# The split steps of a unit in two groups of four and five instead of three groups: a two-layer interaction network on Trainium2

## The reference

```
x0 = e                                                    # B, 39, 16
z0 = einsum('bid,bjd->bdij', x0, x0)    -> B, 16, 39*39
cur0 = relu(z0 @ W0)                    -> B, 128, 16     # W0: 1521 x 128
next_h, direct0 = split(cur0, 2)        # 64 rows each
z1 = einsum('bid,bjd->bdij', x0, next_h) -> B, 16, 39*64
cur1 = relu(z1 @ W1)                    -> B, 128, 16     # W1: 2496 x 128
z = sum(concat([direct0, cur1]), over the 16)
h = relu([z, dense_ctx] @ W_top1 + b_top1); h = relu(h @ W_top2 + b_top2); y = h @ W_top3
```

## Time and profile before

| | |
|---|---|
| runs | 1511.45, 1515.13, 1517.09 us |
| profiled execution | 1511.94 us; span 1510.1 us |
| busy: TensorE, VectorE, ScalarE, GpSimd | 95%, 92%, 55%, 62% |
| mean granted TensorE clock | 0.979 (below 1 only in the first slices) |
| chain that ended last | TensorE 90%, VectorE 4% |

### The profile page before, as it was taken

One profiled execution on the slowest core, in us unless ns is written; L12 is line 12 of the kernel. 1 busy time (PEld: TensorE's weight loads), 2 busy tenths in 40 slices (PEclk: granted clock), 3 DMA queues, 4 the chain that ended last, 5 costly groups with the idle time before them and its releaser, 6 DMA issues.

```text
span 1510.1 us, 15015 instructions
## 1 busy us (share of the span) xinstructions
PE 1434.6 (95%) x4458; PEld 794.5 (53%) x4458; DVE 1393.3 (92%) x1253; ACT 825.2 (55%) x897; POOL 939.0 (62%) x604
## 2 busy tenths in 40 slices
PE   3179999999999999999999999999999999999999
PEld 2145555555555555555555555555555555555556
DVE  2179999999999999999999999999999999999993
ACT  0155555655655555655655555655655555655555
POOL 7638888868687786868687786868687780000000
PEclk7589999999999999999999999999999999999999
DMA  5069989999989899999989999899998998898510
GB/s 150 6 160 203 227 216 218 206 220 212 221 198 222 206 217 214 208 223 201 220 203 216 214 212 220 208 213 203 212 216 223 212 210 216 204 222 207 170 35 1
DMA packets 137289, 293.08 MB, mean 194 GB/s; under 512 B 37646, under 2 KB 62878, under 8 KB 137080
## 3 DMA queue, kind: packets, MB, share of 16 engines
q1 hardware_dynamic: 102642, 278.48, 77.2%
q0 software_dynamic: 19200, 4.95, 2.9%
q10 hardware_dynamic: 15366, 8.70, 2.1%
HBM read 284.08 MB, written 7.87 MB: 193 GB/s over the span
## 4 chain that ended last, share of the span: by engine, by line
PE 90%; DVE 4%; issue 2%; another core or an unknown queue 2%; ACT 0%; DMA 0%; DVEq 0%; SPq 0%
PE psB L493 42%; PE psA L493 14%; PE psB L511 7%; PE psB L514 6%; PE psB L518 6%; PE psA L501 2%; PE psA L511 2%; PE psA L514 2%; PE psA L518 2%; PE psB L501 2%; DVE z L902 1%; PE psA L485 1%; DVE z_lo L911 1%; DVE z_split L902 1%
## 5 line engine op out<-in xcount | busy, mean ns | idle before, releaser
L472 POOL DMA_INDIRECT emb<-in_tbl,ids_all x600 | 938.8, 1565 | 309.7 <-issue 178.9
L493 PE MATMUL psB<-z,w 128*128 128x512 f32 x1544 | 690.1, 593 | 5.3 <-DVE z L902 5.3
L767 ACT ACTIVATE z_hi<-z_split 128x1024 fp32r<-128x1024 f32 (+1 forms) x286 | 301.4, 1057 | 464.9 <-DVE z_split L902 372.4
L493 PEld LDWEIGHTS psB<-z,w 128*128 128x128 f32 x1544 | 292.4, 190 | 362.7 <-issue 346.0
L902 DVE TENSOR_TENSOR z<-h_quad,x_lay 128x1024 f32<-128x1024 f32 x354 | 420.5, 1218 | 7.4 <-PE psB L493 5.4
L911 DVE TENSOR_TENSOR z_lo<-z_split,z_hi 128x1024 fp32r<-128x1024 f32 (+1 forms) x286 | 349.3, 1221 | 6.3 <-ACT z_hi L767 3.2
L902 DVE TENSOR_TENSOR z_split<-h_quad,x_lay 128x1024 f32<-128x1024 f32 x222 | 268.4, 1221 | 0.0
L720 ACT ACTIVATE h_quad<-psA 32x1024 f32<-32x1024 f32 x248 | 251.7, 1015 | 6.1 <-DVE feat_side L987 2.4
L493 PE MATMUL psA<-z,w 126*128 126x512 f32 x512 | 241.9, 594 | 0.0
L511 PE MATMUL psB<-z_hi,w_hi 128*128 128x512 f32 x444 | 157.7, 436 | 0.0
L493 PEld LDWEIGHTS psA<-z,w 126*128 126x128 f32 x512 | 97.3, 190 | 98.4 <-issue 92.7
(11 more groups left out here) (113 smaller groups left out, 862.5 us busy)
## 6 DMA issues: line engine op xcount, KB each, us to landing
x_lay<-x_rows SPq DMA_DIRECT2D x1152, 128.0 KB
x_more<-x_rows SPq DMA_DIRECT2D x62, 504.0 KB
bases<-x_rows SPq DMA_DIRECT2D x62, 468.0 KB
x_lay<-x_rows SPq DMA_DIRECT2D x64, 256.0 KB
x_ring<-x_rows SPq DMA_DIRECT2D x31, 504.0 KB
emb<-in_tbl,ids_all POOLq DMA_INDIRECT x600
x_last<-x_rows SPq DMA_DIRECT2D x64, 128.0 KB
x_rows<-x_side ACTq DMA_DIRECT2D x58, 120.0 KB
```

The costliest lines, as they stand in the source:

```text
L472: nc.gpsimd.indirect_dma_start(emb[t % 2][:, f * D:(f + 1) * D], None, tables[f], bass.IndirectOffsetOnAxis(ids_all[:, t, f:f + 1], 0)).th ...
L493: mm = nc.tensor.matmul(ps[:, cs], w[0:k, :], z[WHOLE_NO[place] % NZ][0:k, cs], start=first, stop=last)
L767: nc.scalar.activation(z_hi[n % NS][0:k, 0:cols], z_split[n % NS][0:k, 0:cols], ACT.Copy).then_inc(z_hi_made, 1)
```

## The change

Only constants change. The steps that are split, and two places of layer 0:

```diff
-SPLIT0 = (1, 4)
+SPLIT0 = (1, 5)
 HALF1 = 12
-SPLIT1 = (2, 3, 7, 8, 9, 13, 14)
+SPLIT1 = (2, 3, 4, 8, 9, 10, 11)
 WHOLE0 = tuple(s for s in range(STEPS0) if s not in SPLIT0)
-EARLY = (2, 3)
+EARLY = (2, 3, 4)
 WHOLE1 = tuple(s for s in range(STEPS1) if s not in SPLIT1 or s in EARLY)
 ORDER0 = SPLIT0 + WHOLE0
-AFTER = (0, 1, 3, 5, 7, 9, 11)
+AFTER = (0, 1, 4, 5, 7, 9, 11)
 FIRST_AFTER = (1, 3, 4, 5, 7, 9, 11)
```

## The result

The changed kernel takes 1570.51 us in the median of four runs (1568.58 to 1598.4) against 1516.11 us (1511.45 to 1526.23): ratio 1.0345, 95% interval 1.0278 to 1.0412. It is slower by 54 us. The profiled execution took 1572.18 us, 60.2 us above the profiled one of before.

What follows compares the result with a forecast made beforehand. TensorE was taken to bound the kernel, without a gap in its 42.5 us units. Waits of 1.47 and 0.55 us a unit, taken as 1.92, gave 55.7 us over 29 units, 57 in all: 1571 us, range 1548 to 1588.

Steps and rivals of the forecast that it cites:

- first wait: At step 4, TensorE waits for parts delayed by ScalarE's two stores: 1.47 us a unit, 1.36 at the lower end.
- first rival: ScalarE's high part of step 4 is not held by the stores; +12 to +17, 1530 us; chance 0.06.
- group of five: Second group, five split steps: fourth low part costs 0.2 us, fifth 0.36 more; together 0.55 us a unit.
- cut from 2.02 to 1.92 us a unit: Sum of both waits per unit, taken as 1.92 because the 0.1 us extras need not all come.
- open weight load: On TensorE after a real wait: a weight load that nothing hid, costing another 0.1 us.
- boundaries at nothing: Between groups of split and whole steps: changing between fp32 and fp32r costs TensorE 0, so one group fewer saves nothing.
- exit from the half steps: Behind the two half steps, an fp32 step now follows: no change taken, between 0.12 us saved and 0.06 us more.
- second rival: Faster: exit into an fp32 step hides its weight load, 0.12 us in 31 units; lead suffices everywhere; 1511 us; chance 0.03.
- third rival: No change: TensorE has room and makes the waits good, weight loads busy only 53%; 1515 us; chance 0.03.
- fourth rival: Worse: later products hold back loads and VectorE loses lead; 1 us more a unit, 1603 us; chance 0.06.
- Unit 1: Unit after the start, where the lead is short: 0.5 us added to the sum.

Runs made afterwards that it cites:

- e1: Changed kernel with ScalarE's high part of step 4 put ahead of keep_x (copy and two stores): unit 42.84 us, 1485.42 us, ratio 1.0063 to before.
- e6: Changed kernel with only keep_x's two stores moved behind the high part of step 4, the copy staying ahead: unit 42.84 us, ratio 1.0070 to before.
- e7: Changed kernel with one more copy of 120 x 512 into a scratch tile ahead of the stores in 29 units: unit 44.97 us, ratio 1.0505 to before.
- e10: Changed kernel with five z buffers instead of four, ScalarE's queue as in the change: unit 44.47 us, 1572.15 us, ratio 1.0388 to before.
- e8: Changed kernel with step 4's high part ahead of keep_x and five z buffers instead of four: unit 42.43 us, ratio 0.9988 to before.
- e5: Changed kernel regrouped to three, one and five split steps, none behind the stores: unit 42.74 us, 1483.98 us, ratio 1.0054 to before.
- e9: Kernel before with five z buffers instead of four as the whole edit: unit 42.47 us, 1512.55 us, ratio 0.9998 to before.
- e4: Kernel before with its nine split steps in seven groups instead of three: unit 42.74 us, 1483.09 us, ratio 1.0053 to before.
- e3: Changed kernel with groups of four, four and one, and step 4's high part ahead of keep_x: unit 42.51 us, 1476.64 us, ratio 1.0000 to before.

## Why the prediction was right

**The place and the size of the first wait.** The working gave 1.47 us between where step 4 was due and the next step; the trace has 1.46. It had the high part starting behind the stores, 3.12 us after the transposes begin (1012.69 - 1009.57); it starts at 1056.14 - 1053.02 = 3.12. e1 and e6 show that the stores are the cause, e7 that the price follows the hold, e10 that lead does not touch it. The first rival, stores that do not hold the next activation, is refuted by these.

The changed kernel's own trace shows the same without any edit. In five of its units the two stores took longer than the usual 1.75 us: 2.24, 2.18, 1.99, 2.40 and 2.05 us in units 9, 11, 12, 13 and 16. Just these units are longer than 44.47 us: 44.95, 44.90, 44.70, 45.12 and 44.77. Each excess of the stores is one of the unit, to 0.02 us. In unit 13:

```profile
697.60 2.40 ACTq L702 DMA_DIRECT2D x_rows<-x_side  x2
700.10 1.06 ACT L767 ACTIVATE z_hi<-z_split 128x1024 fp32r<-128x1024 f32 x1 [2.53 <-PE psB L518]
```

In the kernel before, the stores of one unit took 2.34 us, and that unit lasted 42.52 us: nothing that is due stands behind them there.

**The group of five.** The working gave 0.20 and 0.36 us, together 0.55. It came out of the lead at the group's entry, 5.33 us by the working; the trace has 5.32, from VectorE's first product of the group (1064.05) to where TensorE turns to it (1059.07 + 6 x 1.717 = 1069.37). The low parts at 1074.51 and 1076.24 are late, by 0.07 and 0.22 us, with some 0.1 us behind each. The group takes 7.52 us from there to the half steps; in e8, where its five steps are free, it takes 6.97: 0.55 us. That the first part is the stall's doing and the second the fifth step's is what e1 shows (0.34 us left). The price in a kernel without the stall, 0.36, was the lower end of the working; e1 measured 0.34 and e5 0.24.

**The cut from 2.02 to 1.92 us a unit was wrong.** I took 1.92 because the 0.1 us of the open weight load need not come each time. It came each time. Against e8, the same order with neither wait, the changed kernel loses 1.49 us at step 4 and 0.55 in the group of five, 2.04 us a unit in all, and the working had 2.02. The unit grew by 1.97, since e8's is 0.07 us shorter than that of the kernel before, which the forecast did not have; 0.03 to 0.04 of that also comes in e9 with the fifth buffer alone. That the time came out at 1570.5 where 1571 was said is luck in part: the profile is 60.2 us above its like where 57 were forecast, and the medians are 54.4 apart.

**The boundaries at nothing.** Right: 0.00 us in e4. And the exit from the half steps into an fp32 step costs what it cost into a split one: 1.821 us for the first whole step against 1.717, 0.10 us, where it was 1.495 against 1.384, 0.11. That left the second rival no more than 0.01 us of its 0.12.

**The room on TensorE.** The third rival took the weight loads' busy share, 53% before, as a sign of room. There was none: TensorE had no idle time before, and each wait went through to the end. After the change the share reads 50%, where it was 53%, and the time is 3.5% longer.

**The late loads.** The fourth rival took loads of x that come late in every unit. They do not: from 400 to 1300 us VectorE waits for no load at all. It waits for x_lay once, 1.57 us, at 158.09 us, which is in unit 1. The longer units between 2 and 29 are those of the longer stores, shown above.

**Unit 1** was forecast at 0.5 us above the 1.9 of the others and came at 4.2, 1.8 us more than that. By the starts on TensorE, the late load costs 1.57 us at step 2, and step 4 costs 2.53 us where it costs 1.46 elsewhere. TensorE had been busy for only 3.02 of the 5.00 us from 158 on, and for the products of step 4 the granted clock fell to 0.53 of full, near the lower of its two levels (1.2 GHz; busy times, clock, DMA share and GB/s as above):

```profile
164.60:167.20 2.60, 2.58 (x6) 2.09 (x7) 2.60 (x3) 0.88 (x1) 1.99 (x3) 0.53 0.92 240
```

They took 2.64 us from the first start to the next step, not 1.38, and the whole step behind them 2.17, not 1.72. The kernel before holds the full clock there. Against this stand 0.77 us that unit 1 of the kernel before loses at the fourth low part of its second group, a wait that its other units do not have. The forecast had neither the load nor the clock.

## What to carry to other kernels

When an instruction that others wait for moves in a written-out order, look at what its engine has at the new place, the DMAs that it issues included: 0.86 us of issue each, which the busy shares leave out, was the price here. Compare then the time at which it can start with the time at which its result is due. A group of steps that a helper engine does more slowly than the main one costs nothing until its lead is used up and its deficit from there on (0.24 to 0.36 us for a fifth split step here), so know the lead at the entry to the group, and what caps it; and where a boundary has no cost, fewer and longer groups only spend lead.

## What the runs showed of the hardware

Issuing a DMA on ScalarE's queue holds the next activation for 0.86 us (0.857 in the median of the 58 after); two of them took up to 2.40 us instead of 1.75 in five units, and the next activation was held for that long. Why they took longer is open. Two equal activations behind each other start 0.49 us apart, at 0.60 us each (e7). A product that TensorE really waited for starts 0.05 to 0.06 us after its operand is done (1058.46 to 1058.51 in the unit shown), and the next step comes 0.1 us later than it would (0.56 us, not 0.46). Between fp32 and fp32r matmuls there is no cost (3.10 us for a step of each next to each other, and 3.10 apart, e4). The same kernel takes 1476 us in two series and 1512 to 1516 in the others. The difference lies ahead of unit 1: its transposes come at 158.0 us in the trace of the kernel before (1512 us) and at 121.6 in that of e3 (1476 us), and both have units of 42.5 us from there on. In the second of the 40 slices of the span the DMA engines move 6 GB/s in the slower one and 179 in the faster. Chip 8 has a series of either kind, so the chip alone does not decide it; the cause stays open.
